# Sampling loop of a four-layer image kernel: step size, B and C from one product and three row groups, with the softplus sum and its followers at other places

## Chip, cores and metric

One Trainium2 chip, one of its cores. The time is device microseconds of one launch. Engines by the profile's names: PE (matrix products), PEld (its weight loads), DVE, ACT, POOL, SP (issues the DMAs).

## What is computed

The input is x, four images of 64 channels by 128 by 128, fp32. Four layers each add to x; a group norm stands in front of each. The change is in the third, a two-dimensional selective scan. After two depthwise convolutions and an offset prediction it samples the image bilinearly at the shifted places and then runs a scan over the pixels:

```
xd  = dcn_sample(xc, offset)                 # 4 taps per pixel and group
dts, B, C = split(x_proj_w @ xd, [8, 1, 1])  # rows of one projection
delta = softplus(dt_w @ dts + dt_b)
h[t] = exp(delta[t] * A) * h[t-1] + delta[t] * B[t] * xd[t]
y[t] = C[t] * h[t] + Ds * xd[t]
x   = x + out_proj_w @ layer_norm(y)
```

delta has 64 rows per image; B and C have one row each, that multiplies all 64 channels.

## The kernel before

Two images lie side by side in the 128 partitions (64 channels each), so the whole program runs twice, once per pair. All the layers work on X, which stays in SBUF. The sampling and the scan are one software pipeline over 32 tiles of 4 image rows (512 pixels, one PSUM bank in fp32). Its order is written out by hand: `sample_and_scan_pe` (L1052), `sample_and_scan_dve` (L831), `sample_and_scan_act` (L982) and `sample_and_scan_pool` (L922) each have a `step` for tile c, in which work for earlier tiles (c-1 to c-4) and for c+2 is mixed in; `on(d)` says that tile c+d exists. Every engine executes its list in order and waits on semaphores. `straight` (L794) writes the steps -2 to 35 out one after the other; another branch, for offsets beyond the 3 by 3 neighbourhood (`far`), isn't taken with these inputs.

One tile, before the change:

- PE makes nine selections (`spread(q)`, L1066, bf16) that copy the weights of one tap into all channels, into two banks in turn. `spread(q)` waits until DVE has used selection q-2. DVE's `product(q)` (L856) multiplies selection q by the shifted image. Four of the nine products are summed by PE (`add_up`, L1074), five by POOL (`add`, L948). ACT's copy L1035 makes of the sum the sampled tile XS.
- For tile c-1: PE multiplies XS by WZ (L1105, dt_w times the 8 rows of x_proj_w, folded together once at the start), by WB (L1111) and by WC (L1115), the rows of B and C repeated for all channels, into the banks ZB, BB, CB. ACT makes the parts of the softplus from ZB: absolute value, relu, exponential, logarithm (L1025, L1027, L1028, L1030). DVE's sum L907 makes delta (RL) of them, the last thing in its step. ACT's exponential L1048 makes DA = exp(delta A), POOL's product L977 makes UU = delta xd.
- For tile c-2: DVE multiplies UU by B (L875), scans (L881), multiplies by C (L892) and adds Ds xd (L897).
- For tiles c-3 and c-4: layer norm and output projection (PE L1082, L1090, L1092; ACT L999, L1020, L1022), then DVE's scaling L863 and the update of x L867.

In order, DVE's step is: product 0, L863, product 1, L867, product 2, L875, product 3, L881, product 4, L892, product 5, L897, products 6, 7, 8, L907. PE's is: selections 0 and 1, L1082, selection 2, sum 0, selection 3, sum 1, selection 4, L1090, L1092, sum 2, selection 5, L1105, selection 6, sum 3, selection 7, L1111, selection 8, L1115. An fp32 product of 128 by 128 by 512 shows as two passes in the profile.

At the start (L1169 on) DVE, ACT and PE prepare weights; SP (L486) loads them, waits for ACT's last preparation (L504) and then saves a routing table and four rows of zeros in DRAM (L505 to L508). ACT and POOL wait for these saves (`rt_saved`) before the first layer. After the scan SP stages rows for the fourth layer (`stage`, L554), once the last delta is there (L586).

A place in the program that already has products on 32 rows of PE is `logits` (L2197, in the first layer): they go in turn to different groups of 32 rows, and into different banks.

## Time and profile before

| | |
|---|---|
| median of 3 runs | 2433.34 us (2430.43 to 2440.91) |
| the profiled execution | 2439.82 us, span of its instructions 2438.0 us |
| busy share of the span | PE 88%, DVE 75%, ACT 58%, POOL 58% |
| mean granted PE clock | 0.929 |
| sampling loops, by their first and last selection | 743.3 to about 1088 us and about 1943 to 2282 us |

A row of a timeline has the start in us from the span's start, the duration in us, the engine, the line, the operation, what it writes and reads, the shapes and a count, and in brackets the idle time of the engine before it and who ended it. Instructions of one engine overlap by the length of its pipeline, so what an instruction costs in a packed row is the distance from its start to the next one's, not its duration.

### The profile page before, as it was taken

To read this page: it belongs to the slowest core of one execution; us is meant where nothing else is said; L and a number is where in the kernel's file an instruction comes from. 1 tells how busy PE (TensorE), PEld (TensorE's weight loads), DVE (VectorE), ACT (ScalarE), POOL (GpSimd) and SP (SyncE) were. 2 spreads that over 40 slices of the span, in tenths; PEclk is the share of its full clock that TensorE was granted. 3 is DMA by queue.
4 is the path that set the end of the run, shared out by engine and by line. 5 is a ranking of instruction groups with operands and counts; after the bars stand their busy time and mean duration, and the time that the engine had idled before them with its cause. 6 is when DMAs were issued, how large, how long until landed. Compare 5 with 4: busy or idle time off the path is not lost. (4 is left out here: it accounts for less than half of the span.)

```text
span 2438.0 us, 28756 instructions
## 1 busy us (share of the span) xinstructions
PE 2135.2 (88%) x7363; PEld 1102.2 (45%) x7363; DVE 1834.2 (75%) x3128; ACT 1416.5 (58%) x2192; POOL 1417.2 (58%) x1305
## 2 busy tenths in 40 slices
PE   2998759798998999997988978698989799999798
PEld 2397435443553444433335954353435434444243
DVE  6555667499986999995755658566999589999754
ACT  1843444286884777763346437235868667777532
POOL 2233009398967989972322410484989499999532
PEclk9978879899998999998998979799989799999899
DMA  5000283500001212224820006534000022223244
GB/s 189 1 1 0 92 302 94 199 1 1 1 1 28 44 39 61 40 52 141 251 45 0 1 1 233 189 107 158 0 1 1 12 27 53 48 44 61 83 122 113
DMA packets 199339, 172.78 MB, mean 71 GB/s; under 512 B 72535, under 2 KB 175327, under 8 KB 195831
## 3 DMA queue, kind: packets, MB, share of 16 engines
q1 hardware_dynamic: 199159, 170.78, 24.8%
q8 instruction: 64, 1.05, 0.2%
q14 instruction: 116, 0.95, 0.1%
HBM read 81.69 MB, written 72.29 MB: 63 GB/s over the span
## 5 line engine op out<-in xcount | busy, mean ns | idle before, releaser
L948 POOL TENSOR_TENSOR BIG<-BIG 128x512 f32<-128x512 f32 x320 | 407.1, 1272 | 88.4 <-DVE BIG L856 78.4
L856 DVE TENSOR_TENSOR BIG<-PSUM,BIG 128x512 f32<-128x512 f32 x576 | 391.0, 682 | 59.0 <-PE PSUM L1066 30.7
L1138 DVE SCALAR_TENSOR_TENSOR PSUM<-BIG,VECS,PSUM 128x1024 f32<-128x1024 f32 x224 | 288.2, 1287 | 44.6 <-PE PSUM L2111 39.5
L1074 PE MATMUL PSUM<-BIG,CSTS 128*128 128x512 f32 x512 | 266.8, 602 | 0.0
L782 POOL TENSOR_TENSOR BIG<-TOEP,BIG 128x384 f32<-128x384 f32 x84 | 98.2, 1196 | 270.5 <-DVEq L1543 270.5
L2111 PE MATMUL PSUM<-BIG,WDW 128*128 128x512 f32 x512 | 236.4, 607 | 11.1 <-ACT BIG L2011 11.1
L1066 PE MATMUL PSUM<-BIG,SELB 120*128 120x512 bf16 x576 | 212.0, 386 | 16.7 <-issue 6.8
L2307 PE MATMUL PSUM<-BIG 128*128 128x381 f32 (+1 forms) x576 | 189.5, 493 | 12.9 <-DVE BIG L789 12.9
L1066 PEld LDWEIGHTS PSUM<-BIG,SELB 120*128 120x128 bf16 x576 | 55.3, 96 | 264.4 <-DVE BIG L856 190.9
L2111 PEld LDWEIGHTS PSUM<-BIG,WDW 128*128 128x128 f32 x512 | 99.3, 195 | 141.1 <-issue 122.4
L1784 POOL TENSOR_TENSOR BIG<-BIG 128x1024 f32<-128x1024 f32 x64 | 151.1, 2360 | 10.3 <-POOL BIG L1787 10.3
L2307 PEld LDWEIGHTS PSUM<-BIG 128*128 128x128 f32 x576 | 111.4, 194 | 90.5 <-ACT BIG L1962 13.5
L741 PE MATMUL PSUM<-BIG,WL 128*128 128x512 f32 x256 | 120.9, 617 | 15.2 <-POOL BIG L726 12.3
L725 POOL TENSOR_TENSOR BIG<-BIG 128x576 f32<-128x576 f32 x32 | 38.8, 1214 | 152.9 <-issue 92.6
L1074 PEld LDWEIGHTS PSUM<-BIG,CSTS 128*128 128x128 f32 x512 | 98.2, 195 | 58.6 <-issue 54.2
L1787 POOL TENSOR_SCALAR BIG<-BIG,VECS,CSTS 128x1024 f32<-128x1024 f32 x96 | 114.3, 1197 | 17.1 <-DVE PSUM L1593 11.2
L741 PE MATMUL PSUM<-BIG,WMID 128*128 128x512 f32 x256 | 115.3, 593 | 0.2 <-DVE BIG L716 0.2
L1972 ACT ACTIVATE BIG<-PSUM,SMG 128x1152 f32<-128x1152 f32 x32 | 39.1, 1221 | 121.7 <-PE PSUM L2307 108.4
L1793 POOL TENSOR_TENSOR BIG<-BIG 128x1024 f32<-128x1024 f32 x32 | 75.6, 2362 | 55.5 <-ACT BIG L1999 55.1
L1025 ACT ACTIVATE BIG<-PSUM,VECS 128x512 f32<-128x512 f32 x64 | 44.0, 687 | 108.4 <-PE PSUM L1105 108.4
L1999 ACT ACTIVATE BIG<-BIG,VECS 128x1024 f32<-128x1024 f32 x96 | 102.9, 1139 | 0.0
L1549 DVE SCALAR_TENSOR_TENSOR BIG<-BIG,SMG 128x1152 f32<-128x1152 f32 x32 | 54.2, 1693 | 54.6 <-ACT BIG L1972 54.6
(363 smaller groups left out, 5079.6 us busy)
## 6 DMA issues: line engine op xcount, KB each, us to landing
spill<-X SPq DMA_DIRECT2D x18, 1024.0 KB, 6.1
back_spill<-BIG SPq DMA_DIRECT2D x32, 576.0 KB, 3.4
X<-x SPq DMA_DIRECT2D x32, 512.0 KB, 7.5
rows_spill<-X SPq DMA_DIRECT2D x64, 256.0 KB, 4.1
out<-BIG SPq DMA_DIRECT2D x64, 256.0 KB, 3.6
BIG<-rows_spill SPq DMA_DIRECT2D x28, 512.0 KB, 5.3
X<-back_spill SPq DMA_DIRECT2D x14, 896.0 KB, 12.8
BIG<-fc SPq DMA_DIRECT2D x8, 1024.0 KB, 10.0
```

The costliest lines, as they stand in the source:

```text
L741: ins = pe.matmul(PSUM[:, 4 * k + m, :].rearrange("p (r j) -> p r j", r=8), w, VC[:, k, m, b:b + 8, :], start=(b == 0), stop=(b == 1))
L782: eng.tensor_tensor(to.rearrange("p (x c r) -> p x c r", x=3, r=WROW), TOEP[:, y].unsqueeze(1).unsqueeze(1).broadcast_to([P, 3, WCH, WROW] ...
L856: dve.tensor_tensor(img(product_buffer(b, q)), img(PSUM[:, (k + q) % 2, :]), pch(c, XBASE, dy, dx), ALU.mult).then_inc(df_p, 1)
L948: pool.tensor_tensor(a, a, x, ALU.add).then_inc(df_add, 1)
L1066: pe.matmul(img(PSUM[:, (k + q) % 2, :]), SELB[:, q, :], WTB[0:WROWS, k, :, h, :], start=True, stop=True).then_inc(df_w, 1)
L1074: pe.matmul(PSUM[:, ACC, :], ident, product_buffer(b, m), start=(m == 0), stop=(m == PE_SUMS - 1)).then_inc(df_acc, 1)
L1138: return dve.scalar_tensor_tensor(out=rows8(to), in0=strip(c, base, dy, dx), scalar=vc(weights, j), in1=rows8(acc), op0=ALU.mult, op1=ALU.add)
L1784: pool.tensor_tensor(d_side[:, c % 2, :], d_side[:, c % 2, :], d_tap, ALU.add).then_inc(d1_part, 1)
L1787: pool.tensor_scalar(rows8(d_tap if n else d_side[:, c % 2, :]), strip(c, XBASE, dy, dx), vc("dw_w", DW2_SIDE[n]), cs("zero")[:, 0:1], ALU ...
L1999: act.activation(rows8(a_side[:, j, c % 2, :]), strip(c, BASE, dy, dx), ACT.Identity, scale=vc("conv2d_w", j)).then_inc(d1_side, 1)
L2111: ins = pe.matmul(img(acc[:, h * CH:(h + 1) * CH]), w[:, j - stored, :], strip(c, base, dy, dx)[:, h * ROWS:(h + 1) * ROWS, :], start=(j = ...
L2307: ins = pe.matmul(to, WIDE[:, u % RING, x, :], v, start=(x == 1), stop=(x == 2))
```

## The change

The folded WZ and the repeated WB, WC are gone. WX holds the 10 rows of x_proj_w for each of the two images, three times over, 32 columns apart; WG holds, in rows 0 to 31, dt_w for the 8 rows of dts, in rows 32 to 63 ones for the row of B, in rows 64 to 95 ones for the row of C. PE multiplies XS by WX at the place of L1105 and into the same bank ZB; ACT copies 96 rows of the result to AB; PE then makes step size, B and C by three products with 32 rows each, from rows 0, 32 and 64 of AB, into ZB, BB and CB, behind selection 8. The sums of the tile are the same up to rounding.

- PE's step ends: selection 5, WX, selection 6, selection 7, sum 3, selection 8, the three row groups.
- ACT's copy stands ahead of L1035; the four softplus operations move from there to the end of ACT's step, and DA to its start, one step later.
- DVE's sum for delta moves from the end of its step to behind product 1 of the next step; the product by B and the scan move behind product 4.
- POOL's UU moves behind `add(3)`.
- SP issues six more small DMAs (the rows of WG) before it saves the routing table; the load of the old weights goes. Its stages for the fourth layer wait for the last WX product and not for the last delta.

```diff
-        WQ, WK, WV, WPROJ, WIN, WZ, WB, WC = (sb(n, [P, P]) for n in
-            ("WQ", "WK", "WV", "WPROJ", "WIN", "WZ", "WB", "WC"))
+        WQ, WK, WV, WPROJ, WIN, WX = (sb(n, [P, P]) for n in ("WQ", "WK", "WV", "WPROJ", "WIN", "WX"))
+        WG = sb("WG", [3 * 32, P])
...
-            sp.dma_start(DTS[:, :], dts).then_inc(load, 16)
...
             sp.wait_ge(const_act, 3)
+            for s in range(2):
+                at, cols = s * XR, slice(s * C, (s + 1) * C)
+                sp.dma_start(WG[at:at + DT_RANK, cols], dts[:, 2 * C:3 * C]).then_inc(load, 16)
+                for r in (1, 2):
+                    row = r * 32 + at + DT_RANK + r - 1
+                    sp.dma_start(WG[row:row + 1, cols], cst[0:1, CST["one"][0]:CST["one"][0] + C]).then_inc(load, 16)
             sp.dma_start(rt_spill, RT).then_inc(rt_saved, 16)
...
-                sp.wait_ge(sc_delta, pair * NT + (NT + CREDIT))
+                sp.wait_ge(sc_xd, pair * NT + (NT + CREDIT))
...
                 product(1)
+                if on(-2):
+
+                    dve.wait_ge(sc_ln, after(T - 2))
+                    dve.wait_ge(sc_u, after(T - 3))
+                    dve.wait_ge(sc_da, after(T - 3))
+                    dve.tensor_tensor(RL, PSUM[:, ZB, :], AB, ALU.add).then_inc(sc_delta, 1)
                 if on(-4):
                     dve.wait_ge(sc_t, after(T - 4))
...
                 product(2)
+                product(3)
+                if not far:
+                    product(4)
                 if on(-2):
 
                     dve.wait_ge(sc_u, after(T - 2))
-                    dve.wait_ge(sc_bc, after(T - 2))
+                    dve.wait_ge(sc_zbc, all_three(T - 2))
                     dve.tensor_tensor(PSUM[:, BB, :], UU, PSUM[:, BB, :], ALU.mult).then_inc(sc_bx, 1)
-                product(3)
-                if on(-2):
                     dve.wait_ge(sc_bx, after(T - 2))
...
-                if on(-1):
-
-                    dve.wait_ge(sc_ln, after(T - 1))
-                    dve.wait_ge(sc_u, after(T - 2))
-                    dve.wait_ge(sc_da, after(T - 2))
-                    dve.tensor_tensor(RL, PSUM[:, ZB, :], AB, ALU.add).then_inc(sc_delta, 1)
...
+                if on(-2):
+
+                    act.wait_ge(sc_delta, after(T - 2))
+                    act.wait_ge(sc_h, after(T - 3))
+                    act.activation(DA, RL, ACT.Exp, scale=SM[:, 9:10]).then_inc(sc_da, 1)
...
                 if on(-1):
-                    act.wait_ge(sc_z, after(T - 1))
-                    act.activation(AB, PSUM[:, ZB, :], ACT.Abs, bias=vc("dt_b")).then_inc(sc_abs, 1)
...
+
+                    act.wait_ge(sc_xd, after(T - 1))
+                    act.wait_ge(sc_delta, after(T - 2))
+                    act.activation(AB[0:3 * 32, :], PSUM[0:3 * 32, ZB, :], ACT.Copy).then_inc(sc_copied, 1)
...
                 if on(-1):
-
-                    act.wait_ge(sc_delta, after(T - 1))
-                    act.wait_ge(sc_h, after(T - 2))
-                    act.activation(DA, RL, ACT.Exp, scale=SM[:, 9:10]).then_inc(sc_da, 1)
+                    act.wait_ge(sc_zbc, all_three(T - 1))
+                    act.activation(AB, PSUM[:, ZB, :], ACT.Abs, bias=vc("dt_b")).then_inc(sc_copied, 1)
+                    act.wait_ge(sc_copied, copied(T - 1, 1))
+                    act.activation(PSUM[:, ZB, :], PSUM[:, ZB, :], ACT.Relu, bias=vc("dt_b"))
+                    act.activation(AB, AB, ACT.Exp, scale=-1.0).then_inc(sc_exp, 1)
+                    act.wait_ge(sc_exp, after(T - 1))
+                    act.activation(AB, AB, ACT.Ln, bias=1.0).then_inc(sc_ln, 1)
...
-                    pe.matmul(PSUM[:, ZB, :], WZ[:, :], XS[:, (k + 1) % 2, :], start=True, stop=True).then_inc(sc_z, 1)
+                    pe.matmul(PSUM[:, ZB, :], WX[:, :], XS[:, (k + 1) % 2, :], start=True, stop=True).then_inc(sc_xd, 1)
                 spread(6)
+                spread(7)
                 if not far:
                     add_up(3)
-                spread(7)
-                if on(-1):
-                    pe.matmul(PSUM[:, BB, :], WB[:, :], XS[:, (k + 1) % 2, :], start=True, stop=True)
                 spread(8)
                 if on(-1):
+
+                    pe.wait_ge(sc_copied, copied(T - 1, 0))
                     pe.wait_ge(sc_y, after(T - 2))
-                    pe.matmul(PSUM[:, CB, :], WC[:, :], XS[:, (k + 1) % 2, :], start=True, stop=True).then_inc(sc_bc, 1)
+                    settle(pe)
+                    for r, bank in enumerate((ZB, BB, CB)):
+                        rows = slice(r * 32, r * 32 + 32)
+                        pe.matmul(PSUM[:, bank, :], WG[rows, :], AB[rows, :], start=True, stop=True).then_inc(sc_zbc, 1)
...
-            for w in (WQ, WK, WV, WPROJ, WIN, WOUT, WZ, WB, WC):
+            for w in (WQ, WK, WV, WPROJ, WIN, WOUT, WX, WG):
                 dve.memset(w[:, :], 0.0)
...
-            for s in range(2):
-                p, q = s * C, s * C + C
-                dve.tensor_copy(WZ[p:q, p:q], PSUM[p:q, 0, 0:C])
...
-            pe.matmul(PSUM[:, 0, 0:C], DTS[:, 0:2 * C], DTS[:, 2 * C:3 * C], start=True, stop=True)
```

## Rows read from the trace of the kernel before

**Rows 1.** Windows: a stretch, then busy time of PE, PEld, DVE, ACT, POOL, PEclk, DMA

```profile
790.00:1080.00 290.00, 289.48 (x776) 118.81 (x775) 278.94 (x455) 213.20 (x446) 261.82 (x292) 1.00 0.24 46
```

**Rows 2.** One line's instructions (L907, first pair's loop): durations, first and last start

```profile
L907 DVE TENSOR_TENSOR BIG<-PSUM,BIG x27: 679/680/681, 794.9 to 1077.4; 128x512 f32<-128x512 f32 x27
```

**Rows 3.** Timeline of DVE through one tile: product 2 to the next tile's product 2

```profile
960.97 0.69 DVE L856 TENSOR_TENSOR BIG<-PSUM,BIG 128x512 f32<-128x512 f32 x1
...
966.39 0.68 DVE L856 TENSOR_TENSOR BIG<-PSUM,BIG 128x512 f32<-128x512 f32 x1
967.27 0.69 DVE L856 TENSOR_TENSOR BIG<-PSUM,BIG 128x512 f32<-128x512 f32 x1 [0.20 <-POOL BIG L948]
968.17 0.69 DVE L856 TENSOR_TENSOR BIG<-PSUM,BIG 128x512 f32<-128x512 f32 x1 [0.21 <-PE PSUM L1066]
968.78 0.68 DVE L907 TENSOR_TENSOR BIG<-PSUM,BIG 128x512 f32<-128x512 f32 x1
969.38 0.68 DVE L856 TENSOR_TENSOR BIG<-PSUM,BIG 128x512 f32<-128x512 f32 x1
...
971.84 0.68 DVE L856 TENSOR_TENSOR BIG<-PSUM,BIG 128x512 f32<-128x512 f32 x1
```

**Rows 4.** Timeline of PE in the same tile: selections 4 and 8, products WZ, WB, WC

```profile
961.71 0.39 PE L1066 MATMUL PSUM<-BIG,SELB 120*128 120x512 bf16 x1
...
964.74 1.02 PE L1105 MATMUL PSUM<-BIG,WZ 128*128 128x512 f32 x2
...
966.89 1.02 PE L1111 MATMUL PSUM<-BIG,WB 128*128 128x512 f32 x2
967.75 0.38 PE L1066 MATMUL PSUM<-BIG,SELB 120*128 120x512 bf16 x1
967.97 1.02 PE L1115 MATMUL PSUM<-BIG,WC 128*128 128x512 f32 x2
968.83 0.59 PE L1066 MATMUL PSUM<-BIG,SELB 120*128 120x512 bf16 x2
```

**Rows 5.** Timeline of PE in the first layer: 128-row passes, then passes on 32 rows

```profile
246.34 0.27 PE L2210 MATMUL PSUM<-CSTS,BIG 128*128 128x128 f32 x1
246.54 0.48 PE L2197 MATMUL PSUM<-BIG 32*128 32x256 f32 x2
...
246.86 0.60 PE L2197 MATMUL PSUM<-BIG 32*128 32x256 f32 x4
...
247.29 0.38 PE L2197 MATMUL PSUM<-BIG 32*128 32x256 f32 x2
247.60 0.33 PE L2210 MATMUL PSUM<-CSTS,BIG 128*128 128x128 f32 x1
```

**Rows 6.** Timeline of ACT in the tile of Rows 3: softplus's first, the copy, DA

```profile
965.79 0.69 ACT L1025 ACTIVATE BIG<-PSUM,VECS 128x512 f32<-128x512 f32 x1 [1.44 <-PE PSUM L1105]
...
968.29 0.58 ACT L1035 ACTIVATE BIG<-PSUM 128x512 f32<-128x512 f32 x1
...
969.49 0.72 ACT L1048 ACTIVATE BIG<-BIG,SM 128x512 f32<-128x512 f32 x1
```

**Rows 7.** Timeline of ACT and DVE behind the loop's last tile

```profile
1094.62 0.69 ACT L1025 ACTIVATE BIG<-PSUM,VECS 128x512 f32<-128x512 f32 x1 [1.76 <-PE PSUM L1105]
...
1097.23 0.69 DVE L907 TENSOR_TENSOR BIG<-PSUM,BIG 128x512 f32<-128x512 f32 x1 [2.90 <-ACT BIG L1030]
...
1103.01 0.75 DVE L897 SCALAR_TENSOR_TENSOR BIG<-BIG,VECS,PSUM 128x512 f32<-128x512 f32 x1 [0.96 <-PE PSUM L1092]
```

**Rows 8.** Timeline of POOL in the tile of Rows 3: UU

```profile
970.94 1.28 POOL L977 TENSOR_TENSOR BIG<-BIG 128x512 f32<-128x512 f32 x1
```

**Rows 9.** Timeline at the start: the last save's issue, then ACT, which waits

```profile
52.69 0.60 SPq L508 DMA_DIRECT2D rows_spill<-CSTS  x1
...
54.81 1.28 ACT L1858 ACT_TABLE_LOAD   x1 [5.07 <-DMA rows_spill<-CSTS]
...
56.63 0.26 ACT L1852 ACTIVATE SM<-PSUM,GNE 128x1 f32<-128x1 f32 x1 [0.54 <-PE PSUM L2105]
```

More of the change, by code:

```diff
@@ L31 @@
 DT_RANK = 8
+XR = DT_RANK + 2
 PW = W + 2
@@ L882, in step @@
                                            ALU.mult, ALU.add).then_inc(sc_h, 1)
-                if far and on(-1):
-                    if on(0):
-                        dve.wait_ge(df_acc, summed(T, PE_SUMS - 1, PE_SUMS))
-                    dve.wait_ge(df_add, summed(T - 1, POOL_SUMS - 1, POOL_SUMS))
-                    far_dve(dve, c - 1, (k + 1) % 2, reach)
-                product(4)
+                if far:
+                    if on(-1):
+                        if on(0):
+                            dve.wait_ge(df_acc, summed(T, PE_SUMS - 1, PE_SUMS))
+                        dve.wait_ge(df_add, summed(T - 1, POOL_SUMS - 1, POOL_SUMS))
+                        far_dve(dve, c - 1, (k + 1) % 2, reach)
+                    product(4)
                 if on(-2):
@@ L1173, in _ @@
             dve.reg_mov(far_dve_turn, 0)
-            dve.wait_ge(load, 16 * 9)
-            for w in (WQ, WK, WV, WPROJ, WIN, WOUT, WZ, WB, WC):
+            dve.wait_ge(load, 16 * 8)
+            for w in (WQ, WK, WV, WPROJ, WIN, WOUT, WX, WG):
                 dve.memset(w[:, :], 0.0)
@@ L2391, in _ @@
                 keep_busy(BUSY[2], 5)
+                pe.wait_ge(load, 16 * 14)
                 pe.wait_ge(rad_dve, pair * 16 + 16)
```

35 lines of the change are left out of this document (16 added, 19 removed).

## The prediction

> **What bounds the kernel now.** I read the windows of the loop first. In 290 us of the first pair's loop PE is busy for 289.5 us at a granted clock of 1.00, DVE for 278.9, POOL for 261.8, ACT for 213.2 [rows 1]: PE is full, DVE nearly so, and ACT has room. Then the period of a tile: 27 instructions of L907 start from 794.9 to 1077.4 us, so a tile takes 282.5/26 = 10.87 us [rows 2]. The timeline tells what makes it. Product 2 starts at 960.97 us [rows 3]; its end frees the bank for selection 4, which starts 0.74 us later, at 961.71 [rows 4]; from there PE works without a pause to selection 8 at 967.75, 6.04 us; product 8 starts 0.42 us behind that, at 968.17; and DVE goes from it to the next product 2 at 971.84 in 3.67 us [rows 3]. 0.74 + 6.04 + 0.42 + 3.67 = 10.87: the loop is a ring through both engines, in which PE's 6.04 us is the largest part. DVE loses time in it at two places alone: products 6 to 7 take 0.88 us and 7 to 8 take 0.90, where neighbours without a wait are 0.60 apart (968.17 to 968.78, 968.78 to 969.38) [rows 3]. Without these 0.58 us DVE's step would be 10.29 us. That is its floor.
>
> **What PE saves.** An fp32 product of 512 columns costs 0.86 us (966.89 to 967.75), two passes of 0.43, a selection 0.22 (967.75 to 967.97) [rows 4]. Three products, 2.58 us, go; WX, of the same shape, costs 0.86. What three products on 32 rows cost is read from the first layer's [rows 5]. Two passes on different row groups start at 246.54 together, two more at 246.86, the last two of eight at 247.29: eight passes of 256 columns in four pairs. A pair costs (247.29 - 246.86)/2 = 0.215 us, what one such pass would cost alone, since a pass of 128 columns costs half of that, 0.11. The change of shape costs too: 0.09 us on the way in (0.20 from L2210 to L2197, less its pass of 0.11), 0.10 for the second weight load, which isn't hidden (0.32 between the first pairs instead of 0.215), and 0.09 on the way out (0.31 less 0.215). For 512 columns three row groups side by side are two passes of 0.43, plus 0.10, plus 0.18 for both changes of shape: 1.14 us. So PE's work in a tile falls from 10 x 0.86 + 9 x 0.22 = 10.58 to 8 x 0.86 + 1.98 + 1.14 = 10.00 us. That groups share a pass is what I take from these rows; the other end, all passes one behind the other, would cost 6 x 0.43 = 2.58 instead of 0.86.
>
> One rule speaks against it. The Trainium skill, TensorE: Matmul & The Clock Gate, section on packing small matmuls, says that matmuls start and end strictly in program order. By it a product's two passes on one group would hold up the next group's first pass, and three products would take four pass times, not two. The rows have first passes of two groups start together, which is why the sum goes by two; four is a rival below.
>
> **What it puts on the path.** Now step size, B and C come behind selection 8, and selection 8 waits for product 6 (its bank). Before, L1105 stood three selections earlier and the softplus ran beside PE's and DVE's work. The new ring, from product 2:
>
> 1. DVE from product 2 to product 6: the same eight instructions in another order (products 2 to 5, L875, L881, L892, L897), 966.39 - 960.97 = 5.42 us [rows 3].
> 2. Start of product 6 to selection 8: as product 2 to selection 4, 0.74 us [rows 3, 4]. PE has been through WX, selections 6 and 7 and sum 3 by then: the ring by way of PE is worked out below.
> 3. Selection 8 and the change of shape: 0.22 + 0.09 = 0.31 us [rows 4, 5].
> 4. First pass of the row groups to ACT's absolute value: 1.05 us as from L1105 to L1025 (964.74 to 965.79) [rows 4, 6], plus the load of 0.10 and 0.01 for the third group: 1.16.
> 5. ACT's four operations to DVE's sum for delta: 1094.62 to 1097.23, where DVE did nothing but wait for them: 2.61 us [rows 7].
> 6. The sum 0.60, then the update of x: four instructions from 969.38 to 971.84 take 2.46 us, three of them 0.60 each, which leaves 0.66 for L867 [rows 3]. Together 1.26, and product 2 starts.
>
> Sum: 5.42 + 0.74 + 0.31 + 1.16 + 2.61 + 1.26 = **11.50 us, 0.63 more than 10.87**. From the start of product 6 to delta the ring takes 4.82 us; DVE has products 6, 7, 8, 0, L863 and product 1 to do in it, six times 0.60 = 3.6. It waits for the other 1.2: 0.28 ahead of product 7, for POOL as now, and the rest ahead of product 0 and of L907.
>
> Other rings are shorter. By PE from selection 4 to selection 8 without WB: 0.74 + (6.04 - 0.86) + 0.31 + 1.16 + 2.61 + 1.26 = 11.26. By product 0, whose selection now stands behind the row groups: 5.42 + 0.74 + 0.31 + 0.96 (two passes and the load) + 0.09 + 0.42 + (2.46 + 0.60) = 11.00. What is moved and hidden: ACT's copy, 0.58 us like L1035 [rows 6], must be done by the row groups: WX has 0.86 + 0.22 + 0.22 + 0.86 + 0.31 = 2.47 us of PE work until then, and result and copy take 1.05 + 0.58 = 1.63. Behind the copy on ACT stand L1035 and the two part copies, which nothing needs sooner. DA (0.72 [rows 6]) and UU (1.28 [rows 8]) run from delta beside L867, products 2 to 4, which start the product by B 0.60 + 0.66 + 3 x 0.60 = 3.06 us behind delta; delta's 0.68 and UU's 1.28 make 1.96. POOL, with UU between two sums, has 10% to spare at the old period [rows 1] and more at the new one. If that cover went, UU's surplus over 3.06 would come on top.
>
> **The edges.** Behind the last tile nothing covers the chain: WX, copy and row groups put 0.58 + 0.05 + 1.16 = 1.8 us before the absolute value. L897 waits there for another product, 0.96 us [rows 7], which L863, now ahead of the last delta, can release earlier: 0.84 at the least; I take 1.3 per pair, 2.6. SP's stages for the fourth layer may start earlier, but that layer first needs the last update of x: 0. At the start six DMAs are issued ahead of the saves that ACT waits for [rows 9]: 6 x 0.60 = 3.6, less ACT's slack of 0.54, so 3.1 us at most, and 0 at least, since one load, one product and some copies go from the preparation; I take 2.0. Nothing else reads SP's queue then: its next DMA waits for the first layer's end.
>
> **The sum.** 31 intervals between tiles in each pair, 62 x 0.63 = 39.1, with the edges 43.7 us. The profiled execution took 2439.8 us, which would be 2483.5; it stands 6.5 above the median of 2433.3. On the median: **2477 us**. Bounds: without any cost of the change of shape 11.31 us per tile, 62 x 0.44 + 1.7 = 29, or 2462; with it doubled 11.69, 62 x 0.82 + 3.6 + 3.1 = 58, or 2491. Between them I stay at the rows of the first layer, which are the same instructions.
>
> **Rivals.**
>
> - Faster: PE's relief counts and DVE becomes the bound at its floor, 10.29 us. That needs the way from product 6 to delta (4.82 us) to fit into DVE's own six instructions, 3.6 us; the place is L907 behind product 1. Then 62 x -0.58 + 4.6 = -31, 2402 us. For it: PE is full [rows 1] and loses 0.58. Against: 2.61 of the 4.82 is ACT's own time. 0.12.
> - Delta is not late (ACT's part overlaps more than I can see), but product 0 is, behind the row groups: 11.00 us, 62 x 0.13 + 4.6 = 13, 2446 us. 0.10.
> - The row groups don't run side by side, so the change doesn't do what it says: with two more passes, 12.36 us per tile, 62 x 1.49 + 6.3 = 99, 2532 us. Against it: pairs that start together [rows 5]. For it: the rows don't tell in which order the program had these passes. 0.08.
>
> **Numbers.** Forecast 0.70, rivals 0.12, 0.10, 0.08. A change under 0.5%, 12 us, is about what a measurement here can't tell from none. Faster by more: 0.12. Within: 0.07, most of the second rival. Slower: 0.81. The forecast's own range is 2462 to 2491; with the second rival, and something beyond the upper bound, 2440 to 2500 holds 8 in 10; the first and third rival lie outside.
>
> **What would show it.** In the changed loop: a period of L907 near 11.5 us; L907 with an idle time before it that ACT's logarithm ended (some 0.5 us, and product 0 waiting for its selection, about 0.4); the three products on 32 rows within some 1.1 us and with the same start to a hundredth; PE idle ahead of selection 4 for about a microsecond. The row groups at 2 us or more would be the third rival; a period below 10.87 with no wait at L907 the first. A granted clock below 1.00 in the loop, where PE now pauses, would make all of PE's terms too small. ACT's table load at the start should come about 2 us later.

## The result and the profile after

The changed kernel takes **2498.1 us** (median of 4 runs, 2495.0 to 2504.6) against 2434.8 us (4 runs, 2430.4 to 2440.9) for the kernel before beside it: a ratio of 1.026, 95% interval 1.023 to 1.029. It is slower by 63 us. The profiled execution took 2496.3 us, span 2494.4.

| | before | after |
|---|---|---|
| period of a tile in the loop | 10.87 us | 11.90 us |
| first selection to last update of x, pair 1 / pair 2 | 366.55 / 366.52 us | 398.88 / 400.89 us |
| PE busy in the 290 us of [rows 1] | 289.5 us | 260.2 us |
| ACT's table load at the start | 54.81 us | 56.40 us |

The second pair's first selection stands at 1938.0 us in the kernel before and at 1960.2 us in the changed one.

Windows of the changed kernel over the same stretch, with the columns of [rows 1]:

```profile
790.00:1080.00 290.00, 260.21 (x757) 94.90 (x754) 261.83 (x416) 213.80 (x440) 240.92 (x269) 1.00 0.24 45
```

No engine is full any more: PE, DVE and POOL are busy for 6 to 10% less of the time, at the same granted clock of 1.00. Most of that says only that a tile takes 9% longer, so that fewer tiles lie in the window. But PE, which had next to no idle time, now stands idle for 30 us of 290, in a kernel that became slower: a chain through several engines sets the pace. The line of delta, which answers to [rows 2], gives the period, (1078.6 - 793.1)/24 = 11.90 us:

```profile
L883 DVE TENSOR_TENSOR BIG<-PSUM,BIG x25: 691/691/693, 793.1 to 1078.6; 128x512 f32<-128x512 f32 x25
```

The timeline of DVE through one tile answers to [rows 3] (L869 are the products, L876 the scaling of the output, L883 delta, L886 the update of x, L897 the product by B, L901 the scan, L913 the product by C, L918 is Y):

```profile
960.92 1.88 DVE L869 TENSOR_TENSOR BIG<-PSUM,BIG 128x512 f32<-128x512 f32 x3
962.72 0.69 DVE L897 TENSOR_TENSOR PSUM<-BIG,PSUM 128x512 f32<-128x512 f32 x1
963.44 1.28 DVE L901 TENSOR_TENSOR_SCAN BIG<-BIG,PSUM 128x512 f32<-128x512 f32 x1
964.76 0.70 DVE L913 TENSOR_TENSOR PSUM<-BIG,PSUM 128x512 f32<-128x512 f32 x1
965.36 0.68 DVE L869 TENSOR_TENSOR BIG<-PSUM,BIG 128x512 f32<-128x512 f32 x1
965.96 0.74 DVE L918 SCALAR_TENSOR_TENSOR BIG<-BIG,VECS,PSUM 128x512 f32<-128x512 f32 x1
966.62 0.68 DVE L869 TENSOR_TENSOR BIG<-PSUM,BIG 128x512 f32<-128x512 f32 x1
967.50 1.29 DVE L869 TENSOR_TENSOR BIG<-PSUM,BIG 128x512 f32<-128x512 f32 x2 [0.20 <-POOL BIG L963]
969.17 0.69 DVE L869 TENSOR_TENSOR BIG<-PSUM,BIG 128x512 f32<-128x512 f32 x1 [0.39 <-PE PSUM L1086]
...
971.54 0.69 DVE L883 TENSOR_TENSOR BIG<-PSUM,BIG 128x512 f32<-128x512 f32 x1 [0.48 <-ACT BIG L1068]
...
972.82 1.88 DVE L869 TENSOR_TENSOR BIG<-PSUM,BIG 128x512 f32<-128x512 f32 x3
```

PE in the same tile, answering to [rows 4]: selections 4 and 8, the row groups, selections 0 and 1 of the next tile:

```profile
961.67 0.39 PE L1086 MATMUL PSUM<-BIG,SELB 120*128 120x512 bf16 x1 [1.19 <-DVE BIG L869]
...
967.36 0.39 PE L1086 MATMUL PSUM<-BIG,SELB 120*128 120x512 bf16 x1
967.68 1.13 PE L1138 MATMUL PSUM<-BIG,WG 32*128 32x512 f32 x6
968.74 0.60 PE L1086 MATMUL PSUM<-BIG,SELB 120*128 120x512 bf16 x2
```

And ACT's absolute value behind the row groups, the first of the four softplus instructions [rows 6]:

```profile
968.92 0.69 ACT L1063 ACTIVATE BIG<-PSUM,VECS 128x512 f32<-128x512 f32 x1 [0.22 <-PE PSUM L1138]
```

Read along the ring, from product 2: product 6 at 966.62 (5.70 us), selection 8 at 967.36 (0.74), row groups at 967.68 (0.32), absolute value at 968.92 (1.24), delta at 971.54 (2.62), product 2 at 972.82 (1.28). The sum is 11.90 us, the measured period. Of the waits, DVE's 0.48 us ahead of delta is the one on this ring; the 0.39 ahead of product 0 lies beside it.

At the start, SP's issues and ACT's table load, answering to [rows 9]:

```profile
49.51 0.29 SPq L514 DMA_DIRECT2D WG<-dts  x1
...
51.34 0.36 SPq L518 DMA_DIRECT2D rt_spill<-BIG  x1
...
56.40 1.28 ACT L1877 ACT_TABLE_LOAD   x1 [6.91 <-DMA rows_spill<-CSTS]
```

The six new issues take 1.83 us, 49.51 to 51.34, and the table load comes 1.59 us later than before.

Where the 63 us come from: 62 intervals x (11.90 - 10.87) = 63.9 us, the edges of the two loops 2.8 (the loops are 66.7 us longer), the start 1.6, 68.3 together. The two spans differ by 56.4 us only: about 12 us less are in stages that the change doesn't touch. The profiled execution of before is 5.0 us above the median of its runs and that of after 1.9 below, which makes 56.5 into 63.3; the other 5 us are left unexplained. The stretches outside the two loops differ by as much from one profile to the next: over the fourteen profiled kernels of this case, the one ahead of the first loop lasts 735.5 to 746.1 us and the one between the loops 821.8 to 834.6. For this reason single executions are compared below by the period of a tile, from the line of delta (or, where DVE's sum is gone, of ACT's logarithm) inside the first loop; PE's granted clock there is 1.00 in all of them but the first.

### The profile page after: what moved, and what is told of

It is laid out like the page before. It is cut to its first block and busy times, and to the rows that moved or that the text cites. A ratio compares the mean times of both kernels' runs of the same rounds, so it can differ in the third digit from the quotient of the medians.

```text
span 2494.4 us, 29200 instructions
## 1 busy us (share of the span) xinstructions
PE 2116.2 (85%) x7489; PEld 1063.1 (43%) x7489; DVE 1850.6 (74%) x3123; ACT 1459.1 (58%) x2256; POOL 1415.6 (57%) x1305
## 5 line engine op out<-in xcount | busy, mean ns | idle before, releaser
L869 DVE TENSOR_TENSOR BIG<-PSUM,BIG 128x512 f32<-128x512 f32 x576 | 377.5, 684 | 64.5 <-PE PSUM L1086 42.9
L1094 PE MATMUL PSUM<-BIG,CSTS 128*128 128x512 f32 x512 | 264.1, 597 | 0.0
L1094 PEld LDWEIGHTS PSUM<-BIG,CSTS 128*128 128x128 f32 x512 | 98.8, 193 | 40.4 <-issue 32.6
L1047 ACT ACTIVATE BIG<-PSUM 96x512 f32<-96x512 f32 x64 | 37.9, 593 | 119.0 <-PE PSUM L1125 119.0
```

What stands on the lines that cost most here:

```text
L869: dve.tensor_tensor(img(product_buffer(b, q)), img(PSUM[:, (k + q) % 2, :]), pch(c, XBASE, dy, dx), ALU.mult).then_inc(df_p, 1)
L1094: pe.matmul(PSUM[:, ACC, :], ident, product_buffer(b, m), start=(m == 0), stop=(m == PE_SUMS - 1)).then_inc(df_acc, 1)
```

## The experiments

The theory was the ring above. Its rivals: product 0 behind the row groups sets the pace, and delta has slack; the row groups themselves are the cost; or DVE's new order is.

### Delta back behind product 8

```diff
-                if on(-2):
-                    dve.wait_ge(sc_ln, after(T - 2))
...
-                    dve.tensor_tensor(RL, PSUM[:, ZB, :], AB, ALU.add).then_inc(sc_delta, 1)
...
                 product(8)
+                if on(-1):
+                    dve.wait_ge(sc_ln, after(T - 1))
...
+                    dve.tensor_tensor(RL, PSUM[:, ZB, :], AB, ALU.add).then_inc(sc_delta, 1)
```

> One part of the change undone: the sum for delta (line 883 of the changed kernel) goes back to its old place behind product 8; everything else stays. Theory (the ring runs from product 2 by product 6, selection 8, the row groups and ACT's softplus to delta and from there by the update of x to the next product 2): product 0, L876, product 1 and the update now all stand behind the wait for the logarithm. From the changed kernel's timeline: 5.70 + 0.74 + 0.32 + 1.24 + 2.62 us to delta, then 0.60 four times and 0.66 to product 2, 13.68 us per tile; 62 intervals x (13.68 - 11.89) = +111 us on the changed kernel, about 2609 us. Rival (the softplus isn't what sets the period; product 0 behind the row groups is): delta has slack, the period stays at 11.9 us or falls by the 0.5 us that L883 waited, and the time is within 30 us of 2498.

One execution took 2669.7 us; the period is (1068.5 - 790.4)/19 = 14.64 us:

```profile
L922 DVE TENSOR_TENSOR BIG<-PSUM,BIG x20: 690/691/693, 790.4 to 1068.5; 128x512 f32<-128x512 f32 x20
```

Delta on the ring is borne out, and product 0 as the limit falls. But it is about 1 us per tile more than I had counted. In this tile DVE's timeline puts it ahead of products 2 and 3, which wait for PE's sums 0 and 1 (L1094):

```profile
969.71 0.69 DVE L869 TENSOR_TENSOR BIG<-PSUM,BIG 128x512 f32<-128x512 f32 x1 [0.57 <-PE PSUM L1094]
971.46 1.29 DVE L869 TENSOR_TENSOR BIG<-PSUM,BIG 128x512 f32<-128x512 f32 x2 [1.06 <-PE PSUM L1094]
```

and PE's timeline of the same tile tells why the sums are late:

```profile
967.34 0.55 PE L1086 MATMUL PSUM<-BIG,SELB 120*128 120x512 bf16 x1 [2.67 <-DVE BIG L869]
967.68 1.92 PE L1094 MATMUL PSUM<-BIG,CSTS 128*128 128x512 f32 x2
969.39 0.63 PE L1086 MATMUL PSUM<-BIG,SELB 120*128 120x512 bf16 x1
```

A sum takes 969.39 - 967.68 = 1.71 us here, where it took 0.86 before [rows 4]: twice as long. Its windows (columns of [rows 1]) give the granted clock:

```profile
967.30:970.90 3.60, 3.56 (x6) 1.67 (x7) 2.53 (x5) 2.89 (x8) 2.74 (x4) 0.53 0.90 203
```

0.53 of full speed is nearly the lower level, 1.2 GHz, throughout. PE had stood idle for 2.67 us ahead of it; over the window of [rows 1] the mean clock of this run is 0.93. It doesn't fall in every tile. The next tile, from its delta to the one after, kept 1.00:

```profile
981.48:995.40 13.92, 10.96 (x31) 3.84 (x31) 10.75 (x17) 8.73 (x18) 9.87 (x12) 1.00 0.10 20
```

Of the 20 tiles whose delta starts in the window of [rows 1], all with the same idle time of 2.67 us, 8 kept 1.00 and took 13.92 us, near the 13.68 that were counted; the other 12 had a stretch at the lower level and took 14.8 to 15.5. So the miss is the clock for the most part. In the changed kernel PE idles 1.19 us in each tile and keeps 1.00.

### The product by B one place up

```diff
                 product(3)
+                if on(-2):
...
+                    dve.tensor_tensor(PSUM[:, BB, :], UU, PSUM[:, BB, :], ALU.mult).then_inc(sc_bx, 1)
                 if not far:
                     product(4)
                 if on(-2):
...
-                    dve.tensor_tensor(PSUM[:, BB, :], UU, PSUM[:, BB, :], ALU.mult).then_inc(sc_bx, 1)
                     dve.wait_ge(sc_bx, after(T - 2))
```

> DVE's product by B (L897) goes one place up, so that product 4 stands between it and the scan; the scan and the product by C stay neighbours. Same instructions. Theory (the part of the miss that DVE's order explains: an instruction that stands directly behind the one whose result it needs starts later; product by B to scan takes 0.72 us in the changed kernel and 0.60 from there to another instruction): 0.12 us less from product 2 to product 6, all of it on the ring, so a period of 11.77 instead of 11.89 us, 62 x -0.12 = -7 us. Rival (the order costs nothing, the scan waits for DA or UU): the period stays at 11.89, with a wait in front of the scan or of the product by B.

2496.2 us in one execution; period (1075.8 - 793.6)/24 = 11.76 us, 0.14 less than 11.90:

```profile
L883 DVE TENSOR_TENSOR BIG<-PSUM,BIG x25: 691/692/693, 793.6 to 1075.8; 128x512 f32<-128x512 f32 x25
```

DVE's timeline, product by B, product 4, scan, product by C:

```profile
960.70 0.69 DVE L895 TENSOR_TENSOR PSUM<-BIG,PSUM 128x512 f32<-128x512 f32 x1
961.29 0.68 DVE L869 TENSOR_TENSOR BIG<-PSUM,BIG 128x512 f32<-128x512 f32 x1
961.89 1.27 DVE L902 TENSOR_TENSOR_SCAN BIG<-BIG,PSUM 128x512 f32<-128x512 f32 x1
963.20 0.70 DVE L914 TENSOR_TENSOR PSUM<-BIG,PSUM 128x512 f32<-128x512 f32 x1
```

Apart, product 4 follows the product by B at 0.59 us and the scan follows product 4 at 0.60; the product by C, still directly behind the scan, follows it at 1.31. As neighbours the first pair took 0.72 (963.44 - 962.72 above). So a DVE instruction that needs the result of the one before it starts 0.12 us later here, and there was no wait for DA or UU: the theory's part on DVE's order holds. It waits for a semaphore of that instruction too; whether the 0.12 us are due to the data or to the semaphore, no run separates. The saving of 62 x 0.14 = 9 us doesn't show in one execution's total (the two loops are 3.2 us shorter).

The kernel before has both forms. In its loop the three stand apart, and starts follow one another at 0.60, 0.60 and, behind the scan, 1.19 us:

```profile
961.57 0.69 DVE L875 TENSOR_TENSOR PSUM<-BIG,PSUM 128x512 f32<-128x512 f32 x1
962.17 0.68 DVE L856 TENSOR_TENSOR BIG<-PSUM,BIG 128x512 f32<-128x512 f32 x1
962.77 1.27 DVE L881 TENSOR_TENSOR_SCAN BIG<-BIG,PSUM 128x512 f32<-128x512 f32 x1
963.96 0.67 DVE L856 TENSOR_TENSOR BIG<-PSUM,BIG 128x512 f32<-128x512 f32 x1
```

Behind the last tile, where no products are left, the same three stand side by side, at 0.74 and 1.31 us. The dearer price could have been read there:

```profile
1099.30 0.70 DVE L875 TENSOR_TENSOR PSUM<-BIG,PSUM 128x512 f32<-128x512 f32 x1
1100.04 1.28 DVE L881 TENSOR_TENSOR_SCAN BIG<-BIG,PSUM 128x512 f32<-128x512 f32 x1
1101.35 0.70 DVE L892 TENSOR_TENSOR PSUM<-BIG,PSUM 128x512 f32<-128x512 f32 x1
```

### Delta behind product 2

```diff
                 product(1)
-                if on(-2):
...
-                    dve.tensor_tensor(RL, PSUM[:, ZB, :], AB, ALU.add).then_inc(sc_delta, 1)
...
                 product(2)
+                if on(-2):
+                    dve.wait_ge(sc_ln, after(T - 2))
...
+                    dve.tensor_tensor(RL, PSUM[:, ZB, :], AB, ALU.add).then_inc(sc_delta, 1)
                 product(3)
```

> The sum for delta goes behind the update of x and product 2, two places further back. Theory: the logarithm then comes in time, and the ring by product 0 (its selection stands behind the row groups) takes over: 5.70 + 0.60 (delta is now between product 2 and product 6) + about 0.15 (the product by B waits for POOL's UU, which follows delta) + 0.74 + 0.32 + 1.06 + 0.43 from the row groups to product 0 + 2.46 to product 2 = 11.46 us, between 11.3 and 11.6; 62 x -0.43 = -27 us, about 2471 us, still slower than before. First rival (delta's wait isn't on the ring): no change, 11.9 us. Second rival (delta is followed so closely by UU and the product by B that its lateness only moves to the product by B): 11.8 to 11.9 us with an idle time of 0.5 us ahead of L897 that POOL ended.

2492.1 us; period (1069.9 - 791.5)/24 = 11.60 us:

```profile
L889 DVE TENSOR_TENSOR BIG<-PSUM,BIG x25: 677/680/681, 791.5 to 1069.9; 128x512 f32<-128x512 f32 x25
```

At the upper end of what was expected, since the product by B waits longer for UU than the 0.15 that I had put down: it starts 1.48 us behind the start of products 3 and 4 (966.10), two of which need 1.20.

```profile
967.58 0.70 DVE L897 TENSOR_TENSOR PSUM<-BIG,PSUM 128x512 f32<-128x512 f32 x1 [0.20 <-POOL BIG L993]
```

Delta was the tightest ring. The next one, by product 0, stands at 11.60 us in this order; 0.28 of that is the wait for UU, which the changed kernel doesn't have.

### Softplus without Relu, and the start's DMAs behind the saves

```diff
...
-                    dve.tensor_tensor(RL, PSUM[:, ZB, :], AB, ALU.add).then_inc(sc_delta, 1)
+                    dve.scalar_tensor_tensor(out=RL, in0=PSUM[:, ZB, :], scalar=0.0, in1=AB, op0=ALU.max, op1=ALU.add).then_inc(sc_delta, 1)
...
-                    act.activation(PSUM[:, ZB, :], PSUM[:, ZB, :], ACT.Relu, bias=vc("dt_b"))
```

> Two edits far apart. In the loop ACT's Relu goes out of the softplus chain (0.59 us), and DVE's sum for delta takes the larger of the unbiased step size and zero in the same instruction; this leaves out the bias in that part of the softplus. At the start the six new DMAs of SP go behind the saves. Theory (the softplus is on the ring): delta comes 0.6 us earlier, its wait of 0.56 us beyond the usual spacing goes, and the ring by product 0 takes over: 11.89 - 0.56 + 0.05 (the longer instruction) = 11.38 us per tile, 62 x -0.51 = -32 us. Rival (ACT has slack, delta waits for something else): 11.9 us. For the start: ACT's table load, at 54.8 us before and 56.4 in the changed kernel, comes back to 54.0 to 54.9, if the issue of the six DMAs is what moved it; if it was the products and copies around it, it stays at 56.4.

This kernel leaves out the bias in one part of the softplus. 2461.5 us; period (1074.7 - 791.7)/25 = 11.32 us, without a wait ahead of delta (and the longer instruction cost nothing):

```profile
L883 DVE SCALAR_TENSOR_TENSOR BIG<-PSUM,BIG x26: 681/683/684, 791.7 to 1074.7; 128x512 f32<-128x512 f32 x26
```

One ACT instruction of 0.59 us takes 0.58 us out of the period: ACT's chain is on the ring. What is left is the ring by product 0: with the changed kernel's own spacings, 5.70 + 0.74 + 0.32 + 1.06 + 0.43 from product 2 to product 0 and 3.08 from there to product 2 without a wait, it comes to 11.33 us. By this sum it stands 0.57 us behind the ring of delta in the changed kernel. And the table load is back at its old place, or a little ahead of it, so the issue of the six DMAs is what had moved it:

```profile
54.56 1.28 ACT L1876 ACT_TABLE_LOAD   x1 [5.07 <-DMA rows_spill<-CSTS]
```

### Whole products in place of the row groups

```diff
-        WG = sb("WG", [3 * 32, P])
+        WG = sb("WG", [P, 3 * P])
...
-                        rows = slice(r * 32, r * 32 + 32)
-                        pe.matmul(PSUM[:, bank, :], WG[rows, :], AB[rows, :], start=True, stop=True).then_inc(sc_zbc, 1)
+                        pe.matmul(PSUM[:, bank, :], WG[:, r * P:(r + 1) * P], AB, start=True, stop=True).then_inc(sc_zbc, 1)
```

> The three products on 32 rows each become three products on all 128 rows, with the rows of the other groups zero in the weights, so no row groups run side by side and no shape changes. Theory (groups share their passes): PE needs 3 x 0.86 = 2.58 us from the first pass to selection 0 instead of 1.06, product 0 comes that much later and its ring takes over: 5.70 + 0.74 + 0.22 + 2.58 + 0.43 + 3.06 (product 0, L876, product 1, delta, update of x) = 12.73 us per tile, 62 x +0.84 = +52 us, about 2550 us; the absolute value on ACT comes no later than now, since it needs the first product alone. Rival (the row groups gain nothing over whole products, or product 0 isn't near the limit): 11.9 us or below, within 10 us of 2498.

2592.0 us; period (1079.2 - 799.2)/21 = 13.33 us:

```profile
L883 DVE TENSOR_TENSOR BIG<-PSUM,BIG x22: 692/692/692, 799.2 to 1079.2; 128x512 f32<-128x512 f32 x22
```

PE takes 2.58 us from the first pass to selection 0 (969.74 - 967.16), as expected, where the row groups take 1.06:

```profile
967.16 2.74 PE L1137 MATMUL PSUM<-BIG,WG 128*128 128x512 f32 x6
969.74 0.60 PE L1086 MATMUL PSUM<-BIG,SELB 120*128 120x512 bf16 x2
```

I missed by 0.6 us, because I had the absolute value wait for the first product alone; it waits until all three are counted (`all_three`), so the delta ring grew too, by 2.58 - 1.06 less 0.09 for the shape that doesn't change: 11.90 + 1.43 = 13.33. The row groups do share their passes, and that is worth 1.4 us per tile here.

### Row groups ahead of selection 8

```diff
+                if on(-1):
...
+                    for r, bank in enumerate((ZB, BB, CB)):
...
+                        pe.matmul(PSUM[:, bank, :], WG[rows, :], AB[rows, :], start=True, stop=True).then_inc(sc_zbc, 1)
                 spread(8)
-                if on(-1):
...
-                    for r, bank in enumerate((ZB, BB, CB)):
...
-                        pe.matmul(PSUM[:, bank, :], WG[rows, :], AB[rows, :], start=True, stop=True).then_inc(sc_zbc, 1)
```

> In the changed kernel the row groups go ahead of selection 8 instead of behind it. Theory (terms 2 and 3 of the ring, the way from product 6 by selection 8, are on the path): the row groups then start behind sum 3 (its start and 0.86 + 0.09 us, 0.40 earlier than now), softplus and delta come 0.40 earlier, while selection 8 and products 8 and 0 come up to 0.7 us later, which DVE's idle 0.4 + 0.5 us takes up for the most part: a period of 11.5 to 11.7 us, 62 x -0.3 = -18 us, the wait ahead of delta near nothing. Rival (PE's work between selection 4 and the row groups sets them, not selection 8): 11.9 us, since the row groups start no earlier; or, if selection 8 is on the path by itself, above 12 us.

2475.9 us; period (1070.5 - 793.0)/24 = 11.56 us, within the 11.5 to 11.7 expected:

```profile
L883 DVE TENSOR_TENSOR BIG<-PSUM,BIG x25: 691/692/693, 793.0 to 1070.5; 128x512 f32<-128x512 f32 x25
```

The wait moved from delta to product 8, on DVE's timeline:

```profile
964.01 1.29 DVE L869 TENSOR_TENSOR BIG<-PSUM,BIG 128x512 f32<-128x512 f32 x2 [0.59 <-PE PSUM L1086]
```

Both selection 8 and the row groups are wanted at the same moment; whichever goes second is late. The order of the change is the dearer one by 0.34 us.

### DVE's old order

```diff
                 product(2)
-                product(3)
-                if not far:
-                    product(4)
                 if on(-2):
...
                     dve.tensor_tensor(PSUM[:, BB, :], UU, PSUM[:, BB, :], ALU.mult).then_inc(sc_bx, 1)
+                product(3)
+                if on(-2):
...
                     dve.tensor_tensor_scan(HH[:, k, :], DA, PSUM[:, BB, :], SM[:, 12:13] if first else HH[:, 1 - k, CH - 1:CH],
...
-                    product(4)
+                product(4)
```

> Another part of the change undone: in the changed kernel DVE's product by B goes back between products 2 and 3, the scan between 3 and 4 and the product by C between 4 and 5, as they stood before; delta stays ahead of the update of x. Theory: the two neighbours that cost 0.12 and 0.13 us are apart again (0.25 less), but the product by B now stands 1.9 us behind delta and needs POOL's UU, which is ready 2.33 us behind delta (POOL is at its sum 3 until 1.05 us behind it): a wait of about 0.45 us. Period 11.89 - 0.25 + 0.45 = 12.1 us, 62 x +0.2 = +12 us. Rival (the dearer neighbours aren't what makes product 2 to product 6 take 5.70 us instead of 5.42): 12.3 us or more, with a wait of the same 0.45 us. A period below 11.89 would mean that UU isn't late.

2519.4 us; period (1079.2 - 800.9)/23 = 12.10 us, as worked out:

```profile
L883 DVE TENSOR_TENSOR BIG<-PSUM,BIG x24: 690/692/693, 800.9 to 1079.2; 128x512 f32<-128x512 f32 x24
```

DVE's timeline has the wait for POOL in the gap:

```profile
972.63 0.70 DVE L894 TENSOR_TENSOR PSUM<-BIG,PSUM 128x512 f32<-128x512 f32 x1 [0.39 <-POOL BIG L992]
```

So moving the product by B two products back bought more (the wait for UU, which starts it 0.48 us later) than it cost (two dear neighbours). The second price was missing from the prediction, which let the eight instructions cost what they had cost before.

### A two-instruction softplus on the changed kernel

```diff
-                    dve.tensor_tensor(RL, PSUM[:, ZB, :], AB, ALU.add).then_inc(sc_delta, 1)
...
-                    act.activation(AB, PSUM[:, ZB, :], ACT.Abs, bias=vc("dt_b")).then_inc(sc_copied, 1)
+                    act.activation(AB, PSUM[:, ZB, :], ACT.Exp, bias=vc("dt_b")).then_inc(sc_copied, 1)
                     act.wait_ge(sc_copied, copied(T - 1, 1))
-                    act.activation(PSUM[:, ZB, :], PSUM[:, ZB, :], ACT.Relu, bias=vc("dt_b"))
-                    act.activation(AB, AB, ACT.Exp, scale=-1.0).then_inc(sc_exp, 1)
-                    act.wait_ge(sc_exp, after(T - 1))
-                    act.activation(AB, AB, ACT.Ln, bias=1.0).then_inc(sc_ln, 1)
+                    act.wait_ge(sc_u, after(T - 2))
+                    act.wait_ge(sc_da, after(T - 2))
+                    act.activation(RL, AB, ACT.Ln, bias=1.0).then_inc(sc_delta, 1)
```

> The softplus is worked out as Ln(1 + Exp(x + bias)), two ACT instructions whose last writes delta itself; the absolute value, Relu and DVE's sum go. (For arguments beyond 88 this overflows, where the longer form doesn't.) The rest is the changed kernel. Theory: the chain is no longer on the ring, DVE has one instruction less, and the ring by product 0 remains: 11.89 - 0.56 - 0.61 = 10.72 us per tile, 62 x -1.17 = -73 us, about 2425 us, a little under the kernel before. Rival (the row groups behind selection 8 cost the time by themselves, whatever follows them): above 11.3 us.

2455.1 us; period (1071.2 - 791.3)/25 = 11.20 us, above the 10.72 expected and below the rival's 11.3:

```profile
L1061 ACT ACTIVATE BIG<-BIG x26: 630/632/632, 791.3 to 1071.2; 128x512 f32<-128x512 f32 x26
```

Two waits took the place of the one removed, both on DVE's timeline between product 2 and the scan:

```profile
961.19 2.12 DVE L869 TENSOR_TENSOR BIG<-PSUM,BIG 128x512 f32<-128x512 f32 x3
963.46 0.70 DVE L891 TENSOR_TENSOR PSUM<-BIG,PSUM 128x512 f32<-128x512 f32 x1
```

Products 2 to 4 take 2.12 us instead of 1.88: product 3 waits for PE's sum 1, which started only at 960.90. And the product by B starts 2.27 us behind product 2 instead of 1.80: 0.24 of these 0.47 us are product 3's wait, the other 0.23 the wait for UU, which stands behind POOL's sum 3, and that ends at 962.19. Together they are the 0.48 us that the estimate lacks.

### Two versions meant to beat both, and two controls

The first version keeps the short softplus, spreads dependent neighbours apart and puts the row groups behind the next tile's selection 0:

```diff
...
                 spread(0)
+                if on(-2):
...
+                    for r, bank in enumerate((ZB, BB, CB)):
...
+                        pe.matmul(PSUM[:, bank, :], WG[rows, :], AB[rows, :], start=True, stop=True).then_inc(sc_zbc, 1)
                 spread(1)
...
                 spread(8)
-                if on(-1):
...
-                    for r, bank in enumerate((ZB, BB, CB)):
...
-                        pe.matmul(PSUM[:, bank, :], WG[rows, :], AB[rows, :], start=True, stop=True).then_inc(sc_zbc, 1)
```

> A version meant to beat both: the changed kernel with the two-instruction softplus, the row groups behind the next tile's selection 0 instead of ahead of it, DVE's order product 2, 3, product by B, product 4, scan, product 5, product by C, product 6, Y, products 7 and 8 (no instruction directly behind the one that it needs), and the six DMAs of the start behind the saves. Theory: no chain is left on the ring; DVE needs 10.29 - 0.60 = 9.7 us per tile, PE 10.0 us, so PE is the bound at 10.0 to 10.4 us; 62 x (10.2 - 10.87) = -42 us against the kernel before, about 2393 us. Rival (product 1 now waits for its selection behind the row groups, or the product by B for POOL's UU): 10.7 to 10.9 us, no faster than before.

2475.5 us (5 runs), ratio to before 1.016, 95% interval 1.014 to 1.019: 1.6% slower than the kernel before, and above even the rival's figure. The period is (1070.8 - 793.4)/24 = 11.56 us. DVE's timeline shows products 2 and 3 of one tile:

```profile
968.34 0.69 DVE L869 TENSOR_TENSOR BIG<-PSUM,BIG 128x512 f32<-128x512 f32 x1 [0.65 <-PE PSUM L1088]
969.42 0.69 DVE L869 TENSOR_TENSOR BIG<-PSUM,BIG 128x512 f32<-128x512 f32 x1 [0.39 <-PE PSUM L1088]
```

The row groups now delay everything that PE has behind selection 0, so sums 0 and 1 come late, and products 2 and 3, which reuse their buffers, wait 1.04 us together. I had looked at the selections alone.

The second version leaves the row groups behind selection 8 and gives each of the late ones of the earlier runs room (the orders of the three engines, in short; the wait for the scan goes because WX writes a bank that the scan doesn't read):

```diff
- DVE: product 0, scaling, product 1, update, products 2, 3, 4, by B, scan, by C, product 5, Y, product 6
+ DVE: scaling, product 0, product 1, update, product 2, by B, products 3, 4, scan, products 5, 6, by C, Y
- PE: selection 4, mean, WOUT, sum 2, selection 5, wait for the scan, WX, selection 6, selection 7
+ PE: selection 4, mean, sum 2, selection 5, WX, selection 6, WOUT, selection 7
- POOL: sum 3, UU, sum 4
+ POOL: UU, sum 3, sum 4
```

> A second version meant to beat both. As the version with the two-instruction softplus alone, but: UU goes back ahead of POOL's sum 3; WX no longer waits for the scan (it writes a bank that the scan doesn't read); the second product into the output bank (WOUT) goes behind selection 6; DVE's order is scaling of the output, product 0, product 1, update, product 2, product by B, 3, 4, scan, 5, 6, product by C, Y, 7, 8; and the six DMAs of the start go behind the saves. The row groups stay behind selection 8, as in the changed kernel. Theory: the ring that is left runs product 2 to product 6 in 4.2 us (seven starts at 0.60, the scan counting two), product 6 to product 0 in 2.55 to 3.6 (the row groups now wait for Y, two instructions behind product 6), product 0 to product 2 in 1.87, 8.6 to 9.7 us, less than PE's own work of 10.0 us; so PE is the bound at 10.0 to 10.5 us, 62 x (10.25 - 10.87) = -38 us, about 2397 us. Rival (as in the first such version, an order of mine leaves PE waiting: for product 6 ahead of selection 8, or for POOL's last sum ahead of WX): 10.7 to 11.2 us, no better than the kernel before.

2407.4 us (5 runs), **ratio to before 0.989, 95% interval 0.988 to 0.991**: 1.1% faster than the kernel before and 3.6% faster than the changed one, though 10 us above the 2397 expected. Period (1055.0 - 797.0)/25 = 10.32 us, as expected:

```profile
L1062 ACT ACTIVATE BIG<-BIG x26: 630/630/631, 797.0 to 1055.0; 128x512 f32<-128x512 f32 x26
```

The controls tell what of this is due to the change. The kernel before with the short softplus alone:

> The kernel before with the same two-instruction softplus, to tell what of the last version comes from the shorter softplus and what from the spread by row groups. Theory (PE is the bound of the kernel before): DVE's step shrinks by 0.60 us, but PE's own work is 10.58 us per tile, so the period falls from 10.87 to about 10.6, 62 x -0.27 = -17 us, about 2417 us. Rival (PE's work isn't the bound, only DVE's and ACT's latencies are): 10.27 us, 2397 us.

2421.1 us (8 runs), ratio 0.994, interval 0.992 to 0.996; period (1058.2 - 789.5)/25 = 10.75 us, a little above the 10.6 expected, and far from the rival's 10.27: PE is the bound of the kernel before, nearly. With the order of the second version as well, but three whole products:

> The kernel before, with three whole products on 128 rows, but with the two-instruction softplus and with DVE's order, the place of WOUT's product and the freed wait of the version that beat both: that version without the row groups. Theory (row groups do spare PE 0.58 us, and where no chain hangs on them that is a gain): PE's own work of 10.58 us is a floor here, so the period is 10.58 to 10.7 us against 10.32 with the row groups, 62 x 0.26 to 0.38 = 16 to 24 us more, 2423 to 2431 less the changed kernel's longer edges, about 2420 us. Rival (the gain of that version came from the softplus and the order alone): 10.3 us and 2407 us or less.

2416.1 us (6 runs), ratio 0.993, interval 0.991 to 0.995; period (1051.2 - 797.6)/24 = 10.57 us, PE's own work of 10.58 (10 x 0.86 + 9 x 0.22) to a hundredth. The windows of this control, and behind them those of the second version, over 270 us of the loop, with the columns of [rows 1]:

```profile
790.00:1060.00 270.00, 270.00 (x742) 116.61 (x741) 256.54 (x411) 176.21 (x382) 251.98 (x280) 1.00 0.25 49
```

```profile
790.00:1060.00 270.00, 267.83 (x812) 106.92 (x811) 260.46 (x419) 192.21 (x410) 255.84 (x283) 1.00 0.27 50
```

In the control PE is busy for every one of the 270 us, and its starts follow one another at the prices of that sum, so no order of the same work can go below 10.57; the version with row groups does. (The busy share alone wouldn't show it: PE was busy for 289.5 of 290 us in the kernel before, too, at 10.87 us per tile.) The row groups are thus worth 0.25 us per tile once no chain hangs on them. That version's loops are shorter by 1.8 us per pair only (353.0 against 354.8 us, mean of the two), as its edges are longer, and the two intervals against before just meet at 0.991, so by the whole time the two are not clearly told apart.

## Why the prediction was right and where it fell short

Slower was forecast, by this ring, and so it came: the place of delta, the wait in front of it by ACT's logarithm (0.5 forecast, 0.48), product 0 waiting beside it (0.4, 0.39), the row groups in about 1.1 us with a common start (1.06 to selection 0), PE idle ahead of selection 4 (about 1, 1.19) and the clock of 1.00. The time of 2477 us was 21 us too low, within the range of 2440 to 2500 but outside the forecast's own 2462 to 2491. That the range held is in part luck: 2498.1 lies 1.9 us below its upper end, and the 68.3 us counted above, on the median of 2434.8, would make 2503.

Step by step:

1. Product 2 to product 6: 5.42 forecast, 5.70 measured. **This is the step that failed.** "The same eight instructions in another order" was priced as if order cost nothing. In the kernel before a product stood between any two that depend on each other; the change put product by B, scan and product by C one behind the other. That costs 0.12 and 0.13 us (0.72 instead of 0.60, 1.32 instead of 1.19), 0.25 of the 0.28, shown by the run that took one of the pairs apart and by the one that took both. The trace of the kernel before had the price, behind its last tile.
2. Product 6 to selection 8: 0.74, as forecast.
3. Selection 8 and the shape: 0.31, 0.32.
4. Row groups to the absolute value: 1.16, 1.24. The second passes start 0.53 us behind the first, as counted (0.43 + 0.10); from there to ACT it takes 0.70, where [rows 4, 6] give 0.62. In the run with whole products ACT starts 0.63 us behind the last pass (969.31 to 969.94), so the 0.08 goes with the row groups and not with waiting for three products; what makes it, no run tells.
5. ACT's four instructions: 2.61, 2.62.
6. Delta and update: 1.26, 1.28.

The terms that were off make 0.40 us, 62 x 0.40 = 25 us, more than the whole miss. The edges came out right in their sum alone: 2.8 us for both loops against 2.6, but 0.4 in the first pair and 2.4 in the second, where 1.3 was forecast for each; and 1.6 against 2.0 at the start, where an issue to WG takes some 0.3 us, not the 0.60 of a save [rows 9].

The rivals: "faster, DVE the bound at 10.29" failed on the softplus, as was held against it; PE's relief is real (WX takes 0.86 us, the row groups 1.06 and 0.10 for the shape, where three products took 2.58), and it became a gain only in the version whose chain was cut to two ACT instructions and whose order kept the rest out of the way. "Product 0 sets the pace" is the next ring, at 11.32 us in the run without Relu; its figure of 11.00 was too low by the same 0.28 and some hundredths in other terms. In the run that moved delta it stood at 11.60, by the wait for UU. "The groups don't run side by side" fell: with passes that can't share, the ring grew by 1.43 us. The Trainium skill, TensorE: Matmul & The Clock Gate, section on packing small matmuls, has matmuls start and end strictly in program order; the section on why this matters for kernels has distinct row groups run concurrently. This trace agrees with the second: the three first passes start within 0.02 us of each other and the three second ones 0.53 us later, so a product's second pass didn't hold up the next group's first.

The cover for UU held, as forecast: the changed kernel starts the product by B 3.08 us behind delta (1.28 + 1.80), where 3.06 were forecast. More of it is needed than was forecast, since POOL is still at its sum 3 when delta comes: UU lets the product by B start 2.35 us behind delta (972.63 - 970.28 in the run with the old order), not 1.96. By the old order the product by B waited 0.39 us for UU; the change starts it 1.80 us behind product 2, where UU allows 1.08 (972.63 - 971.55 in that run). That is why the dear neighbours, at 0.25, were still better than the old order; with the product by B one place up the first of them goes as well, at 11.76 us per tile.

## What to carry to other kernels

When work is taken off the engine that is the bound, ask first what its results hang on: a cheaper form that comes later in the tile can turn an overlapped chain into the period. Write the ring out instruction by instruction, and price a pair of dependent neighbours on one engine from a place where they already stand side by side, not from the same instructions apart. And look at a saving again once the new wait is known: here the change lost 1.03 us per tile as it was placed, and its row groups gained 0.25 where the softplus was shorter and the orders of three engines made room for it, of which the longer edges left 1.8 us per pair.

## What the runs showed of the hardware

- A DVE instruction that needs the result of the one directly before it started 0.12 us later than one that doesn't (0.72 against 0.60; behind the scan 1.31 against 1.19), with no idle time that the profile puts down to an engine. The second of the two versions, where Y stands directly behind the product by C, has 0.72 there too (969.02 to 969.74). The Trainium skill, VectorE: DVE Perf Modes, section on the DRAIN, measures that a semaphore between DVE instructions costs nothing extra; the rows here differ where the second instruction reads what the first wrote.
- PE's granted clock was 0.53, nearly the 1.2 GHz level, over the 3.60 us behind an idle time of 2.67 us, and a sum took 1.71 instead of 0.86 us. With that same idle time in every tile it fell in 12 of 20 tiles and stayed at 1.00 in 8; with idle times of 1.2 us per tile it stayed at 1.00.
- Three two-pass fp32 products on three row groups take 1.06 us to the next selection, against 2.58 for three on all rows.
